# Moving half of the value products into loop one's last batch, rounding the first tensors on VectorE, and giving the key rows their own order in the last FFN part

## The chip, the cores and the metric

One core of one Trainium2 chip. The metric is the time of the device in microseconds for one launch of the whole program. TensorE is called PE here, VectorE DVE, ScalarE ACT, GpSimd POOL, SyncE SP; SP issues nearly all the DMAs.

## The reference

Two decoder layers on x (8 batches, 512 rows, 256 channels), with a context of 64 rows per batch. All in float32:

```
x = LN(x + linear_attention(x));  x = LN(x + cross_attention(x, ctx))
x = LN(x + FFN(x))      # FFN: up, gate, sigmoid, t and v are rounded to 16 bits,
                        # each by the maximum of its absolute value over ALL 8 batches
x = LN(x + metric_attention(x))
x = LN(x + cosine_attention(x, ctx))   # k, v = ctx @ Wkv; 16 heads of 64; k = l2norm(k) * k_scale
x = LN(spectral(x) + bias)
```

The global maxima divide the program: no value of a tensor can be rounded until the maximum over all batches is known. Two things of the second layer depend on the context alone and are worked out ahead of it: the scaled, normalised keys (`ck_d`, four groups of 128 context rows) and the products of the values with the output weights (`vw_d`). The values come in 8 pairs of heads (`values(p)`), and each pair gives 2 units (`value_products(n)`, n from 0 to 15).

## The kernel before, in words

Every engine runs a list of its own, written out by hand, and the lists meet at semaphores. `unrolled(engine, steps)` takes a list of (skew, step) pairs and in round n calls each step for batch n minus its skew. An engine takes its instructions strictly in the order of the list, and so does SP's queue.

1. **Loop one** (to 367 us): linear and cross attention for the 8 batches. The last rounds hold batch 7 alone: `xat_turn_probs`, `xat_denominators`, `xat_spread`, `xat_values`, `xat_project_o` on PE. Then the three FFN weights are turned (`turn`, L894), while DVE normalises batch 7, finds the maximum of x and rounds x.
2. **Gate pass** (380 to 474 us): x is turned and multiplied with the gate weights, batch by batch (L911, L922).
3. **Up part** (487 to 590 us): `up_pass(u)` on PE; ACT rounds the gate (`gate_round`, L1406), takes the sigmoid (`ffn_sigmoid`, L1411) and copies the up products (L1399); DVE multiplies and looks for maxima (`gate_product`, `t_peak`, `up_peak`). Between them PE works out `values(0)` to `values(2)` and `value_products(0)` to `(5)` (L979, L1000). ACT copies them (`copy_values` L1438, `copy_vw` L1448) into one buffer (`vw_at`, three from unit 11 on), and SP stores each unit in two DMAs (`store_vw`, L560).
4. **Last FFN part** (604 to 692 us): ACT rounds t and up of the batch `V_ORDER[q]` (`ffn_round_t` L1501, `ffn_round_up` L1509), DVE multiplies them and takes the maximum (`product(q)`, L2056 and L2059). SP loads up for q+2 once ACT has rounded q, and stores the product. PE and ACT do `values(3)` to `(7)`, units 6 to 15, and the keys: `key_rows(g)` on PE (L1014), `copy_keys(g)` (ACT, L1520), a square on POOL (L1726), `sum_keys(g)` on DVE (L2068), a power and a product on POOL (L1728, L1731), `turn_keys(g)` on PE (L1022), `store_keys(g)` (ACT, L1531, with its own DMA).
5. **Loop two** (692 us to the end): down projection, metric, cosine and spectral parts for the 8 batches. Before it DVE waits until all the keys are stored, and PE until they are scaled.

The lists of this kernel follow.

## Time and profile before

| | us |
|---|---|
| median of three runs | 1440.66 (1438.76 to 1443.44) |
| profiled execution, its own time | 1441.74 |
| its span | 1439.4 |
| PE busy | 1256.5 (87%) |
| DVE busy | 1039.9 (72%) |
| ACT busy | 518.6 (36%) |
| POOL busy | 274.1 (19%) |

The busy shares are means over parts with different limits. In the row "PEclk" of the page each digit is the clock that PE was granted in a fortieth of the span, in tenths: 9 is the full 2.4 GHz within rounding, and 7 or 6 means that PE spent part of the slice at 1.2 GHz. The low digits lie where loop one ends and in the last FFN part.

### The profile page before, as it was taken

The page shows a single profiled execution, that of the slowest core. Times are in us where ns is not written, and L with a number is a line of the kernel's source. Part 1 is how long each engine was busy: PE and PEld are TensorE (multiplying, and loading weights), DVE is VectorE, ACT ScalarE, POOL GpSimd, SP SyncE. Part 2 cuts the span into 40 slices and gives each one's busy share as a digit, 9 for nine tenths or more (in the row PEclk, how much of TensorE's full clock was granted, in tenths as well). Part 3 has the DMA queues.
Part 4 walks back from the last instruction along what each step waited for, and adds up shares of the span by engine and source line. Part 5 has one row for each costly group of instructions (what it writes and reads, how often), then busy time and mean ns, then how long its engine had stood idle before and what let it go on. Part 6 is the DMA issues. An engine that isn't in the chain of part 4 may idle for free.

```text
span 1439.4 us, 18378 instructions
## 1 busy us (share of the span) xinstructions
PE 1256.5 (87%) x7324; PEld 837.9 (58%) x7324; DVE 1039.9 (72%) x1925; ACT 518.6 (36%) x602; POOL 274.1 (19%) x188
## 2 busy tenths in 40 slices
PE   7899999977699999664568999999999999998964
PEld 4565666655444544332456576867767686766653
DVE  3579889986346488786543597987879797878684
ACT  1234334433234577677011423332233333241410
POOL 0011111110000000054100230414132141414140
PEclk9899999998899999877699999999999999999997
DMA  5000000000251146498220210021111000000000
GB/s 209 15 15 31 30 30 30 16 15 16 106 217 59 74 155 216 146 386 305 91 83 17 92 51 31 30 68 44 52 59 51 30 23 24 29 22 25 1 15 15
DMA packets 47060, 105.23 MB, mean 73 GB/s; under 512 B 10496, under 2 KB 31104, under 8 KB 43648
## 3 DMA queue, kind: packets, MB, share of 16 engines
q1 hardware_dynamic: 42816, 101.96, 20.1%
q10 hardware_dynamic: 4160, 2.10, 0.5%
q8 instruction: 58, 0.95, 0.3%
q14 instruction: 26, 0.21, 0.0%
HBM read 60.01 MB, written 44.04 MB: 72 GB/s over the span
## 4 chain that ended last, share of the span: by engine, by line
PE 74%; DVE 16%; ACT 5%; issue 3%; DMA 1%; POOL 1%; SPq 0%; POOLq 0%; DVEq 0%; ACTq 0%
PE ps L1197 7%; PE ps L1257 7%; PE ps L1086 6%; PE ps L922 6%; PE ps L973 5%; PE ps L733 3%; PE ps L1230 3%; PE ps L1144 3%; PE ps L877 2%; PE ps L1168 2%; PE ps L806 2%; PE ps L1179 2%; PE ps L824 2%; PE ps L1274 2%; PE ps L713 2%
## 5 line engine op out<-in xcount | busy, mean ns | idle before, releaser
L1257 PE MATMUL ps<-arena 128*128 128x256 f32 x512 | 119.9, 389 | 6.7 <-ACT arena L1654 6.7
L1197 PE MATMUL ps<-arena 128*128 128x512 f32 x256 | 117.6, 598 | 0.0
L1257 PEld LDWEIGHTS ps<-arena 128*128 128x128 f32 x512 | 98.7, 195 | 27.8 <-ACT arena L1654 10.2
L1681 POOL TENSOR_TENSOR arena<-arena 128x4 f32<-128x4 f32 x48 | 49.4, 1032 | 340.8 <-DVE arena L1839 340.8
L1086 PE MATMUL ps<-arena 128*128 128x256 f32 x384 | 89.7, 394 | 22.6 <-DVE arena L2100 20.4
L2145 DVE TENSOR_TENSOR arena<-ps,arena 128x2048 f32<-128x2048 f32 x32 | 73.3, 2292 | 39.3 <-PE ps L1144 39.1
L1745 POOL TENSOR_TENSOR arena<-arena 128x16 f32<-128x16 f32 x32 | 91.9, 2906 | 34.1 <-DVE arena L2174 34.1
L1086 PEld LDWEIGHTS ps<-arena 128*128 128x128 f32 x384 | 75.2, 199 | 33.9 <-issue 20.8
L922 PE MATMUL ps<-arena 128*128 128x512 f32 x192 | 86.1, 606 | 1.2 <-ACT arena L1373 1.2
L973 PE MATMUL ps<-arena 128*128 128x512 f32 x192 | 85.0, 596 | 1.4 <-ACT arena L1399 1.4
L1197 PEld LDWEIGHTS ps<-arena 128*128 128x128 f32 x256 | 46.3, 190 | 48.1 <-issue 44.5
L1633 ACT ACTIVATE arena<-ps 128x512 f32<-128x512 f32 x64 | 38.3, 599 | 98.2 <-PE ps L1197 98.2
L1654 ACT ACTIVATE arena<-ps 128x1024 f32<-128x1024 f32 x32 | 32.8, 1026 | 110.3 <-PE ps L1244 110.3
L1845 DVE TENSOR_SCALAR arena<-arena 128x256 f32<-128x256 f32 x192 | 67.4, 416 | 7.0 <-POOL arena L1681 7.0
L1230 PE MATMUL ps<-arena 128*128 128x128 f32 x512 | 63.3, 277 | 6.0 <-DVE arena L2188 6.0
L1688 POOL TENSOR_TENSOR arena<-arena 128x1024 f32<-128x1024 f32 x8 | 18.8, 2353 | 246.6 <-DVE arena L1899 246.6
L1230 PEld LDWEIGHTS ps<-arena 128*128 128x128 f32 x512 | 60.4, 192 | 8.3 <-DVE arena L2188 7.6
L922 PEld LDWEIGHTS ps<-arena 128*128 128x128 f32 x192 | 36.8, 195 | 45.0 <-issue 43.2
L973 PEld LDWEIGHTS ps<-arena 128*128 128x128 f32 x192 | 36.1, 190 | 45.6 <-issue 40.5
L733 PE MATMUL ps<-arena 128*128 128x512 f32 x128 | 59.2, 597 | 1.3 <-ACT arena L1307 1.3
L1992 DVE TENSOR_REDUCE arena<-arena 128x1 f32<-128x3072 f32 (+1 forms) x9 | 26.9, 2994 | 39.6 <-issue 39.6
L1833 DVE BATCH_NORM_STATS2 arena<-arena 128x6 f32<-128x256 f32 x144 | 51.8, 415 | 4.5 <-POOL arena L1688 2.6
(247 smaller groups left out, 2639.0 us busy)
## 6 DMA issues: line engine op xcount, KB each, us to landing
v_scratch<-arena SPq DMA_DIRECT2D x7, 1536.0 KB, 8.8
arena<-v_scratch SPq DMA_DIRECT2D x7, 1536.0 KB, 6.8
up_scratch<-arena SPq DMA_DIRECT2D x6, 1536.0 KB, 7.0
arena<-up_scratch SPq DMA_DIRECT2D x6, 1536.0 KB, 9.7
arena<-x_scratch SPq DMA_DIRECT2D x16, 512.0 KB, 4.0
vw_scratch<-arena SPq DMA_DIRECT2D x32, 256.0 KB, 5.0
arena<-vw_scratch SPq DMA_DIRECT2D x8, 1024.0 KB
arena<-x SPq DMA_DIRECT2D x8, 512.0 KB, 5.5
```

The lines of the kernel that those rows point to most:

```text
L733: last = mm(flat(t % 2), lin_xt[:, par, k, t * P:(t + 1) * P], w["lin_wkv"][:, k], start=k == 0, stop=k == NC - 1)
L922: last = mm(flat(2 + j), wgate_t[:, k, j * P:(j + 1) * P], ffn_xt[:, par, k], start=k == 0, stop=k == NC - 1)
L973: last = mm(flat(2 + n % 4), wup_t[:, k, j * P:(j + 1) * P], ffn_xt[:, u % 2, k], start=k == 0, stop=k == NC - 1)
L1086: last = mm(rows2(5)[:, t], dn_v[:, t, j], wdown_t[:, j], start=j == 0, stop=j == NF - 1)
L1197: last = mm(flat(p % 2), w["cos_wq"][:, k, p * P:(p + 1) * P], xt4[:, k], start=k == 0, stop=k == NC - 1)
L1230: last = mm(flat(0, 2)[:, p * P:(p + 1) * P], cos_q[:, p, t * P:(t + 1) * P], cos_kb[:, par, p], start=True, stop=True)
L1257: last = mm(flat(2)[:, C:2 * C], cos_pt[:, p], cos_vw[:, par, p], start=p == 0, stop=p == NP - 1)
L1681: g.tensor_tensor(var[0], var[1], neghalf[:, 0:NT], ALU.pow)\
L1745: g.tensor_tensor(cos_nn[:, t, 0:H], cos_nn[:, t, 0:H], neghalf[:, 0:H], ALU.pow)\
L1833: v.bn_stats(st[:, t], r[:, t])
L1845: last = v.tensor_scalar(y[:, t], r[:, t], mv[:, t, 0:1], rs[:, t:t + 1], ALU.subtract, ALU.mult)
L2145: v.tensor_tensor(met_s[:, n % 2].rearrange("p r t h n -> p (r t h) n"), flat(3, 4).rearrange("p (h n) -> p h n", n=P), w["causal"].unsque ...
```

## The change

Values 0 to 3 and units 0 to 7 move into loop one's last batch and into the turning of the weights. For them SP loads the context, the value weights, the output weights and one column of `pack_prep` early, into room that loop one's last batch has left; the copies go to three buffers. Values 4 to 6 and units 8 to 13 take the places in the up part that 0 to 2 and 0 to 5 had; values 7 and units 14 and 15 alone are left in the last FFN part. The first gate rounding is done by DVE in two halves, and the sigmoid of batch 0 follows in halves; the first t rounding is done by DVE. The key rows are squared by ACT from PSUM, their banks move by one, and DVE sums them after q = 2, 3, 5, 6. Loop two's waits for the keys move from its head to the first `met_mask_states` (DVE) and the first `met_scores(0)` (PE). The gate weights are turned into the banks that the up weights used, once these are copied.

```diff
-        VW_LATER = 11
+        VW_AHEAD = 8
+        AHEAD_V_BANK = (2, 2, 0, 1)
+        AHEAD_VW_BANK = (0, 0, 4, 4, 2, 2, 2, 2)
         def vw_at(n):
-            return 0 if n < VW_LATER else (n - VW_LATER + 1) % 3
+            return 1 + n % 3 if n < VW_AHEAD else 0
...
# SP, loop one
+            def load_values_ahead(b, par):
+                if b.last():
...
+                    sp.dma_start(null_raw, pack_prep[:, prep_at:prep_at + 2]).then_inc(loaded["pack_prep"], 16)
...
+                    sp.dma_start(early_ctx.rearrange("p a b -> p (a b)"), ctx_d).then_inc(ev("ctx_again_loaded"), 16)
...
+                        sp.dma_start(early_wv[k], pack_wv[:, k * INNER:(k + 1) * INNER])\
...
+                    wait(sp, "lin_q_ready", b)
+                    sp.dma_start(early_wo.rearrange("p a b -> p (a b)"), pack_l1[:, wo_at:wo_at + NP * C])\
...
-            unrolled(sp, [(0, load_x), (3, load_ahead), (3, store_x3)])
+            unrolled(sp, [(0, load_x), (2, load_values_ahead), (3, store_ahead(0, 1, 2)), (3, load_ahead),
+                          (3, store_ahead(3, 4, 5)), (3, store_x3)])
+            store_vw(6)
+            store_vw(7)
# PE, loop one: values_ahead(p) is 2 products of 128x512, products_ahead(n) 4 of 64x256
+                (3, products_ahead(0)), (3, values_ahead(1)), (2, lin_out(3)), (1, lin_project_kv(0)),
...
+                (3, products_ahead(1)), (1, lin_project_kv(2)), (3, xat_denominators), (3, products_ahead(2)), (2, lin_turn_y), (1, lin_project_kv(3)),
+                (2, xat_project_q), (3, xat_spread), (2, xat_scores(0)), (3, products_ahead(3)), (3, xat_values),
+                (3, values_ahead(2)), (2, xat_scores(1)), (3, xat_project_o), (2, xat_turn_probs(0)), (0, lin_turn_x), (2, xat_scores(2)), (1, lin_state),
+                (2, xat_turn_probs(1)), (2, values_ahead(0)), (2, xat_scores(3)), (1, lin_out(0))])
...
             turn(4, "w_up", NF, NC)
-            wait(pe, "xat_out_added", Batch(B - 1))
-            turn(0, "w_gate", NF, NC)
+            values_ahead(3)(final, 1)
+            products_ahead(4)(final, 1)
             pe.wait_ge(ev("weight_copied"), WEIGHTS["w_up"])
+            turn(4, "w_gate", NF, NC)
+            products_ahead(5)(final, 1)
+            products_ahead(6)(final, 1)
+            pe.wait_ge(ev("weight_copied"), WEIGHTS["w_gate"])
             turn(4, "w_down", NC, NF)
+            products_ahead(7)(final, 1)
# ACT: copy_values_ahead and copy_vw_ahead stand behind xat_exp and the copies in the same order
# ACT, first sigmoid
+            def first_sigmoid():
+                half = NF * T // 2
+                act.wait_ge(ev("half_gate_rounded"), 1)
+                f(gated[:, 0, 0:half], gate_i[:, 0, 0:half], ACT.Sigmoid, scale=quant["gate_scale"])\
...
-            gate_round(0)
-            ffn_sigmoid(0)
+            first_sigmoid()
# ACT, last FFN part, whole new list
+            copy_values(7), copy_vw(14), ffn_round_up(0), ffn_round_up(1), copy_vw(15), ffn_round_t(1),
+            ffn_round_up(2), ffn_round_t(2), copy_keys(0), ffn_round_up(3), ffn_round_t(3), ffn_round_up(4),
+            copy_keys(1), ffn_round_t(4), ffn_round_up(5), ffn_round_t(5), store_keys(0), ffn_round_up(6),
+            copy_keys(2), ffn_round_t(6), store_keys(1), ffn_round_up(7), copy_keys(3), ffn_round_t(7),
+            store_keys(2), store_keys(3)
# ACT, copy_keys
+                if g:
+                    act.wait_ge(ev("cos_k_summed"), g)
+                f(ksq, flat(1 + 2 * (g % 2), 2), ACT.Square).then_inc(ev("cos_k_squared"), 1)
# POOL
-                g.tensor_tensor(ksq, row, row, ALU.mult).then_inc(ev("cos_k_squared"), 1)
# DVE
-                wait(dve, "t_rounded", Batch(q))
+                if q == 0:
+                    link(v.tensor_scalar(t_i[:, 0], gated[:, at], quant["t_mult"], None, ALU.mult))
+                else:
+                    wait(dve, "t_rounded", Batch(q - 1))
...
-                if 1 <= q <= 4:
-                    sum_keys(q - 1)
+                if q in (2, 3, 5, 6):
+                    sum_keys((2, 3, 5, 6).index(q))
...
-            dve.wait_ge(ev("ck_stored"), 16 * 4)
# DVE, met_mask_states; PE's wait for cos_k_scaled moves likewise to met_scores(0)
+                if b.first():
+                    dve.wait_ge(ev("ck_stored"), 16 * 4)
```

(The new ACT list is written here with commas; in the file each call has a line.)

## Rows read from the trace of the kernel before

**Rows 1.** Busy time of each engine in the last FFN part, by stretch.
```profile
core 0: us, PE busy (x) PEld busy (x) DVE busy (x) ACT busy (x) POOL busy (x), PEclk, DMA share, GB/s
...
604.22:692.66 88.44, 43.85 (x145) 21.22 (x143) 65.11 (x49) 60.85 (x36) 36.90 (x13) 0.73 0.87 313
```

**Rows 2.** The chain of waits, 600 to 613 us: start, length, what.
```profile
601.45 4.55 ACT arena L1509 x2
...
606.84 2.85 ACT arena L1501
...
609.71 3.36 DVE arena L2056
```

**Rows 3.** Groups by line and shape, 600 to 692 us: busy, mean ns, idle before.
```profile
L2056 DVE TENSOR_TENSOR arena<-arena 128x3072 f32<-128x3072 int16 x8 | 26.9, 3357 | 15.8 <-ACT arena L1501 15.7
L2059 DVE TENSOR_REDUCE arena<-arena 128x1 f32<-128x3072 f32 x8 | 26.8, 3348 | 0.3
L1501 ACT ACTIVATE arena<-arena 128x3072 int16<-128x3072 f32 x8 | 22.8, 2846 | 0.6 <-ACT arena L1531 0.6
L1509 ACT ACTIVATE arena<-arena 128x3072 int16<-128x3072 f32 x8 | 22.7, 2852 | 10.4 <-DVE arena L2056 10.4
L1014 PE MATMUL ps<-arena 128*128 128x512 f32 x32 | 20.3, 793 | 4.3 <-ACT arena L1531 4.3
L1728 POOL TENSOR_TENSOR arena<-arena 128x16 f32<-128x16 f32 x4 | 17.7, 4437 | 6.4 <-DVE arena L2069 6.4
...
L1448 ACT ACTIVATE arena<-ps 128x1024 f32<-128x1024 f32 x10 | 10.2, 1016 | 4.5 <-DMA vw_scratch<-arena 4.4
...
L2068 DVE TENSOR_REDUCE arena<-arena 128x16 f32<-128x1024 f32 x4 | 4.9, 1220 | 9.8 <-POOL arena L1726 9.8
```

**Rows 4.** DMA issues: KB of each, median us from issue to landing.
```profile
v_scratch<-arena SPq DMA_DIRECT2D x7, 1536.0 KB, 8.8
...
arena<-up_scratch SPq DMA_DIRECT2D x6, 1536.0 KB, 9.7
```

**Rows 5.** PE in time, end of loop one: start, length; idle before in brackets.
```profile
290.71 1.95 PE L866 MATMUL ps<-arena 128*128 128x128 f32 x16
...
349.45 1.24 PE L824 MATMUL ps<-arena 128*128 128x128 f32 x8 [2.74 <-ACT arena L1339]
351.81 3.64 PE L842 MATMUL ps<-arena 128*32 128x128 f32 x64 [1.11 <-ACT arena L1346]
356.53 3.78 PE L866 MATMUL ps<-arena 128*128 128x128 f32 x16 [1.08 <-DVE arena L1927]
...
363.69 3.72 PE L877 MATMUL ps<-arena 128*128 128x256 f32 x16 [1.41 <-DVE arena L1933]
...
380.17 1.94 PE L911 MATMUL ps<-arena 128*128 128x128 f32 x8 [8.32 <-DVE arena L1983]
```

**Rows 6.** Busy time by stretch, columns as in rows 1, around loop one's end.
```profile
349.45:367.25 17.80, 14.19 (x121) 10.84 (x122) 4.90 (x5) 2.05 (x2) 2.00 (x1) 0.71 0.24 90
...
380.17:390.93 10.76, 9.59 (x22) 4.88 (x23) 2.66 (x4) 1.02 (x1) 0.00 (x0) 0.64 0.27 98
```

**Rows 7.** PE in time, up part: the first wait, one values, one unit.
```profile
487.34 3.70 PE L973 MATMUL ps<-arena 128*128 128x512 f32 x8 [1.39 <-ACT arena L1399]
...
521.84 1.88 PE L979 MATMUL ps<-arena 128*128 128x512 f32 x4
...
536.98 1.13 PE L1000 MATMUL ps<-arena 64*128 64x256 f32 x8 [1.69 <-ACT arena L1448]
```

**Rows 8.** ACT in time at the first sigmoid.
```profile
481.53 1.28 ACT L1411 ACT_TABLE_LOAD   x1
482.83 2.85 ACT L1411 ACTIVATE arena<-arena 128x3072 f32<-128x3072 int16 x1
```

**Rows 9.** DVE in time, the first scaling of a sigmoid.
```profile
485.78 1.76 DVE L2022 TENSOR_SCALAR arena<-arena 128x3072 uint16<-128x3072 f32 x1 [6.97 <-ACT arena L1411]
```

**Rows 10.** POOL in time, the power of the third key group.
```profile
650.32 2.90 POOL L1728 TENSOR_TENSOR arena<-arena 128x16 f32<-128x16 f32 x1 [1.60 <-DVE arena L2069]
```

More of the change, by code:

```diff
@@ L325, in decoder @@
         kst = ar.take(NP, P)
-        vw_bufs = (vw_out, ar.take(2, 2, C), ar.take(2, 2, C))
+        ar.at = lin_x_at
+        early_wv = [ar.take(INNER)]
+        early_vst = (ar.take(B * TC), ar.take(B * TC))
+        ar.at = lin_xt_at
+        early_wv.append(ar.take(INNER))
+        early_ctx = ar.take(NC, B * TC)
+        ar.at = lin_zq_at
+        early_wo = ar.take(NP, C)
+        ar.at = lin_z_at
+        vw_bufs = [vw_out, ar.take(2, 2, C), ar.take(2, 2, C)]
+        ar.at = lin_ek_at
+        vw_bufs.append(ar.take(2, 2, C))
+        assert keep + 3 * NF * T <= lin_x_at and ar.at <= keep + B * NF * T
+        null_raw = small[:, 42:44]
         ar.at = keep
@@ L863, in xat_spread @@
                 wait_behind(pe, "xat_spread_copied", b, 1, 1, 1)
+                if b.last():
+                    pe.wait_ge(ev("vw_copied"), 2)
                 for c in range(NC):
@@ L879, in xat_project_o, with values_ahead, step @@
                 last.then_inc(sig("xat_out_projected").sem, 1)
+            def values_ahead(p):
+                def step(b, par):
+                    if not b.last():
+                        return
+                    if p == 0:
+                        pe.wait_ge(ev("ctx_again_loaded"), 16)
+                        pe.wait_ge(loaded["pack_wv"], 16 * NC)
+                        wait_behind(pe, "xat_out_added", b, 1, 1, 1)
+                    elif p == 1:
+                        pe.wait_ge(ev("cos_v_copied"), 1)
+                    else:
+                        wait(pe, "xat_spread_copied", b)
+                    for k in range(NC):
+                        last = mm(flat(AHEAD_V_BANK[p]), early_wv[k][:, p * P:(p + 1) * P], early_ctx[:, k],
+                                  start=k == 0, stop=k == NC - 1)
+                    last.then_inc(ev("cos_v_projected"), 1)
+                return step
@@ new lines, in products_ahead, with step @@
+            def products_ahead(n):
+                p = n // 2
+                def step(b, par):
+                    if not b.last():
+                        return
+                    pe.wait_ge(ev("cos_v_copied"), p + 1)
+                    if n == 0:
+                        pe.wait_ge(loaded["pack_l1"], 16)
+                        wait_behind(pe, "xat_spread_copied", b, 1, 1, 1)
+                    elif n == 2:
+                        wait(pe, "xat_shifted", b, NT, NT)
+                    elif n == 4:
+                        wait(pe, "xat_out_added", b)
+                    else:
+                        pe.wait_ge(ev("vw_copied"), n)
+                    for i in range(2):
+                        at = (2 * (n % 2) + i) * P
+                        for r, (lo, hi) in enumerate(((0, CD), (CD, P))):
+                            last = mm(flat(AHEAD_VW_BANK[n] + r)[:, i * C:(i + 1) * C],
+                                      early_vst[p % 2][lo:hi, at:at + P], early_wo[lo:hi, p], start=True, stop=True)
+                    last.then_inc(ev("vw_done"), 1)
+                return step
@@ L918, in step @@
                     for j in range(half * NF // 2, (half + 1) * NF // 2):
-                        if not b.first():
+                        if b.first():
+                            pe.wait_ge(ev("vw_copied"), VW_AHEAD)
+                        else:
                             wait(pe, "gate_copied", b, j + 1 - NF, NF)
@@ L1377, in ffn_copy_gate @@
                 g_b = gated[:, b.off].rearrange("p (t j n) -> p t j n", t=NT, j=NF)
+                if b.off == 3:
+                    for n in range(VW_AHEAD - 3, VW_AHEAD):
+                        act.wait_ge(vw_line(n), 32 * vw_before(n) + 32)
                 for j in range(NF):
@@ L1530, in store_keys @@
                     act.wait_ge(ev("ck_stored"), 16 * g)
-                f(kst.rearrange("p a b -> p (a b)"), flat(2 + 2 * (g % 2), 2), ACT.Copy, scale=gk)\
+                f(kst.rearrange("p a b -> p (a b)"), flat(1 + 2 * (g % 2), 2), ACT.Copy, scale=gk)\
                     .then_inc(ev("cos_k_scaled"), 1)
@@ L2037, in up_peak @@
                 link(v.tensor_tensor(quant["up_max"], quant["up_max"], peaks[:, 0:1], ALU.max))
-            for n in range(B - 1):
+            first_gate_product()
+            t_peak(0)
+            up_peak(0)
+            for n in range(1, B - 1):
                 gate_product(n)
```

279 lines of the change are left out of this document (156 added, 123 removed).

## Prediction

> **What bounds the kernel now.** I read the page's clock row first: PE holds nearly its full clock except where loop one ends and in the last FFN part. Then I cut the span into stages by busy time. In the last FFN part, 88.44 us long, no engine is full: PE 43.85, DVE 65.11, ACT 60.85, and the DMA engines are at 0.87 [rows 1]. The chain of waits says what order does there: ACT rounds two up tensors, then t, and only then does DVE begin its first product at 609.71 [rows 2]. From there to the last maximum DVE needs 8 products (3.357) and 8 maxima (3.348) [rows 3]; yet it is idle 15.8 us before products, for ACT's t rounding, and 9.8 before key sums, for POOL's square [rows 3]. So the stage is held by the order of ACT's list, not by any engine's work.
>
> At the end of loop one PE waits again and again: 2.74 us for an exponential, 1.11, 1.08 and 1.41 after it, and 8.32 before the first turn of the gate pass [rows 5]. It also works at a mean granted clock of 0.71 from 349.45 to 367.25, and 0.64 from 380.17 to 390.93 [rows 6]; 0.5 is 1.2 GHz, 1.0 is 2.4. The same 16 instructions of L866 take 1.95 in the round before and 3.78 here [rows 5].
>
> All terms are set against the profiled execution, 1441.74 (span 1439.4 and 2.3 around it), which stands 1.08 above the median 1440.66.
>
> **Part A, values and units in the drain of loop one.** Added on PE: 4 values at 1.88 (a record's length, of which some 0.16 overlaps the next, so 1.72) and 8 units at 1.13, with the same overlap 1.06 [rows 7]: 4 x 1.72 + 8 x 1.06 = 15.4 us. ACT gets 4 copies of 512 and 8 of 1024 elements; the latter take 1.016 [rows 3]. The former I put at two thirds of that, 0.7; they can't be below 0 nor above 1.016. Together 11 us. Where they fall:
> - values 0, unit 0 and values 1 (4.5 us) lie in the waits for batch 7's exponentials, of which the last alone is 2.74 [rows 5] and the one before it in the same rhythm is as long. Unit 1 lies in the 1.11 before L842, unit 2 in the 1.08 before L866 [rows 5]. Nothing of these on the path.
> - unit 3 stands ahead of `xat_values`, with no wait there to cover it: +1.06. Values 2 (1.72) stands ahead of `xat_project_o`, whose wait for DVE is 1.41 [rows 5]: +0.3.
> - values 3, units 4 to 7 (1.72 + 4.2 = 6.0) and the turns of the gate and down weights lie beside DVE's normalising, the maximum of x and its sharing, 12.7 us from the end of `xat_project_o` to 380.17. Step by step, counting from that end: up weights turned at 1.3, unit 4 at 4.1, gate weights at 5.4, unit 5 at 6.5, unit 6 at 8.9 (after ACT's copies), down weights at 10.2, unit 7 at 11.3, ACT's last copy at 12.6. It fits by 0.1. What is late if it doesn't fit is the first turn, one for one.
> - the clock. Each fall of PE's clock stood behind waits like these. With the waits filled, PE has hardly a gap over 1.5 us until loop one's end, and I take the clock as kept. L842 then takes half of 3.64, -1.8; L866 takes 1.95 for 3.78, -1.8 [rows 5]. So `xat_project_o` comes at 1.06 + 0.3 - 3.6 = -2.2. Likewise for the gate pass's start: 9.59 busy at clock 0.64 is 6.1 at full clock, -3.4 [rows 6]. Part A: -5.6. Bounds: -7 (the copies' room also shortens something), and +2.5 if the clock falls as before (no saving, unit 2 doubles and outgrows its wait by 1.0, +1.4 from above; the 3.4 stays too), up to +6 if the three-buffer chain of copy and store is late as well.
> - SP: the new loads, 2.5 MB, are issued behind batch 5's store and have some 20 us until they are needed; an up load of 1.5 MB lands in 9.7 [rows 4]. The last x3 store comes behind the stores of units 3 to 5, about 3 us later than before, but only batch 7's later load reads it, and the load of batch 2, behind it in the queue, is issued at the first turn as before. Nothing.
>
> **Part B, first gate rounding.** ACT's rounding and its sigmoid go one after the other, with a table load of 1.28 between, and PE's fifth up product then waits 1.39 for ACT's first copy [rows 7, 8]. DVE's half should take half of 1.76 [rows 9], 0.9; then the table, then two half sigmoids of 1.4: ACT is free 1.9 us sooner, PE's wait of 1.39 goes, and PE paces the up part from there. -1.4. Bounds: 0, if the table is loaded late and halves carry a fixed cost; -1.9.
>
> The Trainium skill (ScalarE: Activation LUTs, "What ACT_TABLE_LOAD costs") charges a switch of tables 2.66 us, the load and a drain. Here the sigmoid starts 0.02 after the 1.28 of the load [rows 8]: this trace has no such drain. By the rule Part B would be -0.5, by the row -1.4.
>
> The places of units 8 to 13 in the up part are those of units 0 to 5, with one buffer again: the 1.69 wait per pair [rows 7] stays, no change.
>
> **Part C, the last FFN part.** The head: DVE rounds t of q = 0 itself (1.76 as in [rows 9], while ACT rounds up), so product 0 waits for ACT's first up rounding alone. In the chain two roundings start at 601.45 and 606.84 is where t's began [rows 2]; the first ends at 604.2. 609.71 - 604.2 = 5.5 sooner.
>
> The pace: a round of DVE is 3.36 + 3.35 + 0.16 and gaps = 6.98; eight are 55.8; four key sums of 1.22 and a small one, 1.45 each, are 5.8: 61.6 against the 79.8 that it took from 609.71 to 689.5 (the stage's end at 692.66 [rows 1], less 3.2 for the last scale and roundings). Units 6 to 13 and values 3 to 6 leave ACT (8 x 1.0 + 4 x 0.7 = 11 us), and four squares come to it (L1448's 1.016 is the nearest row, the same shape from PSUM; at least 0, at most 2). ACT's list is then 15 roundings started every 2.75, 41, plus units 14 and 15 and values 7, 8 key copies and squares, 4 scaled stores: 57 in all, under DVE's 61.6. What still stalls DVE: round 3 by the wait of `copy_keys(0)` for v's first store (8.8 [rows 4] from 609), 0.7; the last key group, where `key_rows(3)` (8 x 0.793 = 6.3 at most [rows 3]) waits for `store_keys(1)`, so that t(7) comes 2.4 late; POOL's product, which held a one-element DVE operation for 1.2 in two of the rounds. I put 4.3. So 79.8 - 61.6 - 4.3 = -13.9, and with the head -19.4.
>
> Bounds: with no stall -23.7; with 8 us more of stalls (half of the 15.8 + 9.8 [rows 3] that there were, less what I count) -11.5. The DMA engines move 88.44 x 313 = 27.7 MB [rows 1]; 16 unit stores of 0.26 go, so 23.5 MB are left for 67 us, 350 GB/s. It ran at about that rate. In order of issue the loads for q = 5, 6 and 7 come 1 to 3 us before ACT wants them.
>
> **Part D, the waits of loop two.** The last key store would land some 8 us after `store_keys(3)`, about when DVE ends or 10 us later; its first readers are 40 us into loop two. Moved, it costs 0. Left where it was, it would have cost up to 10, which is why it must be counted with Part C.
>
> Sum: 1441.74 - 5.6 - 1.4 - 19.4 = 1415.3; less 1.08 for the median, **1414**.
>
> **The rivals.**
> 1. *The clock falls at loop one's end all the same.* The work put in is short pieces, and 2.74 and 8.32 were not the only gaps. Against it: those gaps are the ones filled. Part A +2.5 for -5.6: **1422**.
> 2. *DMA paces the last FFN part.* For it: 0.87 busy over the whole stage [rows 1], and a round of 7 to 8 us asks for 1.5 MB in and 1.5 MB out. If it moves 313 GB/s as before, 23.5 MB take 75 us from 604, 8 more than I give: **1422 to 1424**.
> 3. *POOL's power holds DVE's products.* POOL's L1728 took 4.437 in the mean [rows 3] against 2.90 for the third group, which had begun before DVE's product [rows 10]: POOL waits for DVE. The other way round nothing shows: 8 products have a mean of 3.357 [rows 3]. If each of four products waited 2.9, that is 11.6 less the 2.4 counted: **1423**. The Trainium skill (SBUF — State Buffer, "Who interferes with whom") calls the shared port an exclusive lock of whoever starts first, which would bring this about where the power starts first.
> 4. *The key groups run behind DVE's list: slower than before.* `sum_keys(g)` stands in DVE's order, and DVE stops there until ACT has squared the group, which needs a free bank, hence the store of group g-2, hence POOL's power and product of that group. Before, DVE waited 9.8 for four sums [rows 3]. If each group misses its place by more than a round, 26.4 / 4 = 6.6 us beyond what I count is where it decides; at 8.5 us each, +34: **1448**. Against it: from copy to scaled store a group took 16 us, and the places are 7 to 15 us apart with two groups in flight.
> 5. *The moved units don't take anything off the path*, since ACT waited for t in its own order: then only the head and Part B count, 1441.74 - 5.5 - 1.4 - 1.1: **1434**. Against it: the 15.8 us idle ends at ACT's L1501 [rows 3], with unit copies ahead of it in the list.
>
> **How the numbers follow.** My forecast 0.52 (its own range 1410 to 1418), rival 1 0.22, rivals 2 and 3 together 0.14, rival 5 0.04, rival 4 0.03; 0.05 below 1410, where the stalls vanish. 8 in 10: 1408 to 1427. 0.3% of this kernel is 4.3 us, about what its measurement can tell from no change. Faster 0.96, same 0.015, slower 0.025.
>
> **What would show it.** PE's L842 near 1.9 and L866 near 1.95 in batch 7, and a clock near 1.0 from 349 to 390 (Part A, against rival 1); PE's 1.39 wait gone (B); the first L2056 about 5.5 us after the last scale and the eight of them within 66 us; DVE idle before L2056 under 5 us, not named DMA (C, rival 2); L2056 with a mean still 3.36 (rival 3); idle before L2068 under 4 (rival 4); no idle of DVE or PE for the keys in loop two (D). It is wrong if the gate pass starts no sooner than 380, or if the stage from the last up product to loop two is over 80 us.

## The result and the profile after

The changed kernel takes 1428.53 us in the median of four runs (1426.56 to 1429.01), the kernel before, measured beside it, 1442.05 (1438.76 to 1444.49): a ratio of 0.9903, 95% interval 0.9885 to 0.9922. It is faster by 13.5 us. The forecast was 1414, a gain of 26.7, in a range of 1408 to 1427: the direction was right, half of the size is missing, and the time lies outside the range. The profiled execution took 1429.01, span 1427.2, against 1441.74 and 1439.4 before.

First the end of loop one, PE in time (start, length; idle before and what ended it). These rows answer to [rows 5]: L888 is the old L842, L914 the old L866, L927 the old L877, L1012 the old L911 and L1025 the gate pass.

```profile
350.35 1.96 PE L888 MATMUL ps<-arena 128*32 128x128 f32 x64 [0.22 <-ACT arena L1439]
...
353.38 2.05 PE L914 MATMUL ps<-arena 128*128 128x128 f32 x16
...
360.12 3.62 PE L927 MATMUL ps<-arena 128*128 128x256 f32 x16
...
371.84 1.14 PE L968 MATMUL ps<-arena 64*128 64x256 f32 x8 [1.48 <-ACT arena L1472]
...
376.54 1.07 PE L1012 MATMUL ps<-arena 128*128 128x128 f32 x8 [1.05 <-DVE arena L2101]
378.79 7.11 PE L1025 MATMUL ps<-arena 128*128 128x512 f32 x12 [1.17 <-ACT arena L1502]
385.74 1.04 PE L1012 MATMUL ps<-arena 128*128 128x128 f32 x8
```

The clock beside it, by stretch (columns as in [rows 1]; the number after the bracket of POOL is the granted clock). The first stretch answers to the first of [rows 6]: 1.00 instead of 0.71. In the gate pass the clock still fell, two stretches of 2 us show it at 0.71 and at 0.50, the lower level of 1.2 GHz.

```profile
350.35:363.57 13.22, 13.20 (x133) 9.18 (x133) 4.75 (x4) 4.62 (x5) 0.00 (x0) 1.00 0.79 221
...
378.00:380.00 2.00, 1.22 (x2) 0.70 (x3) 0.00 (x0) 0.73 (x1) 0.00 (x0) 0.71 0.84 245
380.00:382.00 2.00, 2.00 (x3) 0.77 (x3) 0.00 (x0) 0.00 (x0) 0.00 (x0) 0.50 0.74 184
```

Then the last FFN part, groups by line and shape from 592 to 678 (busy, mean ns, idle before). L2195 is DVE's product, the old L2056; L2207 the key sum, the old L2068; L1665 ACT's scaled key copy, ahead of its store.

```profile
L2195 DVE TENSOR_TENSOR arena<-arena 128x3072 f32<-128x3072 int16 x8 | 26.9, 3358 | 5.7 <-ACT arena L1632 3.5 <-ACT arena L1640 2.1
...
L2207 DVE TENSOR_REDUCE arena<-arena 128x16 f32<-128x1024 f32 x4 | 4.9, 1219 | 7.5 <-ACT arena L1654 7.4
L1665 ACT ACTIVATE arena<-ps,arena 128x1024 f32<-128x1024 f32 x4 | 4.5, 1114 | 10.7 <-PE ps L1125 6.2 <-DMA ck_scratch<-arena 4.5
```

DVE's idle time before products fell from 15.8 to 5.7, before key sums only from 9.8 to 7.5 [rows 3], and almost all of the latter is one wait of 7.43. DVE in time, product 3 and the last key group:

```profile
621.79 3.36 DVE L2195 TENSOR_TENSOR arena<-arena 128x3072 f32<-128x3072 int16 x1 [1.83 <-ACT arena L1632]
...
661.43 1.22 DVE L2207 TENSOR_REDUCE arena<-arena 128x16 f32<-128x1024 f32 x1 [7.43 <-ACT arena L1654]
```

The chain of waits (start, length, what) says what it hung on:

```profile
597.60 3.36 DVE arena L2195
...
635.59 15.80 DMA ck_scratch<-arena
651.48 1.12 ACT arena L1665
652.65 6.73 PE ps L1117 x8
659.43 0.89 issue
660.32 1.02 ACT arena L1654
661.34 2.75 ACT arena L1632
664.11 3.36 DVE arena L2195
667.51 3.36 DVE arena L2198
670.90 0.17 DVE arena L2199
671.09 0.16 DVE arena L2079
671.25 3.89 issue
675.15 0.39 POOL arena L1824
...
678.00 12.90 PE ps L1177 x48
```

Read it from below. Loop two begins at 678.00 (692.66 before). POOL shares v's maximum at 675.15, 3.9 us after DVE had it, in a pause that the trace puts to nothing ("issue"); before, the share came 0.1 us behind the end of DVE's copy. The last product stands at 664.11 behind ACT's rounding, that behind the square of key group 3, that behind PE's key rows, these behind the scaled copy that `store_keys(1)` begins with, and this behind the landing of the first key store, which took 15.80 us.

Both traces side by side, each stretch after less before. The measured column adds to the change of the span, -12.2, but for rounding:

| stretch | forecast | measured |
|---|---|---|
| loop one to batch 7, the same work in both | 0 | -1.4 |
| Part A, to the second turn of the gate pass (390.77, 385.74) | -5.6 | -3.6 |
| Part B, to the last unit pair of the up part (590.18, 583.49) | -1.4 | -1.7 |
| head of Part C, to the first product (609.71, 597.60) | -5.5 | -5.4 |
| its pace, first product to last maximum (79.8, 73.5) | -13.9 | -6.3 |
| last maximum to loop two (3.15, 6.91) | 0 | +3.8 |
| loop two (746.7, 749.2) | 0 | +2.5 |

### The profile page after: what moved, and what is told of

It is laid out like the page before. It is cut to its first block, busy times and chain, and to the rows that moved or that the text cites. A ratio compares the mean times of both kernels' runs of the same rounds, so it can differ in the third digit from the quotient of the medians.

```text
span 1427.2 us, 18392 instructions
## 1 busy us (share of the span) xinstructions
PE 1249.9 (88%) x7324; PEld 832.9 (58%) x7324; DVE 1042.0 (73%) x1930; ACT 516.8 (36%) x605; POOL 263.7 (18%) x184
## 4 chain that ended last, share of the span: by engine, by line
PE 74%; DVE 15%; ACT 4%; issue 3%; DMA 2%; POOL 1%; SPq 0%; POOLq 0%; DVEq 0%; ACTq 0%
PE ps L1290 8%; PE ps L1350 7%; PE ps L1177 6%; PE ps L1025 6%; PE ps L1076 6%; PE ps L779 3%; PE ps L1323 3%; PE ps L1237 3%; PE ps L927 2%; PE ps L1261 2%; PE ps L852 2%; PE ps L1272 2%; PE ps L1367 2%; PE ps L870 2%; PE ps L1337 2%
## 5 line engine op out<-in xcount | busy, mean ns | idle before, releaser
L1025 PE MATMUL ps<-arena 128*128 128x512 f32 x192 | 85.5, 602 | 1.2 <-ACT arena L1502 1.2
L1025 PEld LDWEIGHTS ps<-arena 128*128 128x128 f32 x192 | 36.5, 193 | 44.6 <-issue 42.9
```

The lines of the kernel that those rows point to most:

```text
L1025: last = mm(flat(2 + j), wgate_t[:, k, j * P:(j + 1) * P], ffn_xt[:, par, k], start=k == 0, stop=k == NC - 1)
```

## The experiments

The runs of one kernel lie up to 8 us apart (e11_all, 1410.84 to 1418.75), and in the traces the first batches of loop one, which are the same in all, end up to 5 us apart: the unit behind PE's wait of 1.48, at 371.84 above, stands between 368.80 and 374.07 in the eleven traces that have it besides. I call its start the mark. Beside the median (of four runs; of two for e3_thin_v) I read the distance from this mark to the first product and to the first down projection of loop two, and the length from there to the end:

| kernel | median us | ratio to before, 95% | first product | loop two | its length |
|---|---|---|---|---|---|
| changed kernel | 1428.53 | 0.9885 to 0.9922 | 225.8 | 306.2 | 749.2 |
| e1_two_stages | 1419.83 | 0.9808 to 0.9853 | 226.7 | 300.8 | 748.5 |
| e2_share_first | 1433.64 | 0.9909 to 0.9956 | 226.2 | 312.0 | 747.9 |
| e3_thin_v | 1423.89 | 0.9839 to 0.9893 | 225.9 | 300.7 | 748.5 |
| e5_pool_square | 1427.8 | 0.9865 to 0.991 | 225.8 | 306.9 | 749.4 |
| e6_gate_act | 1428.81 | 0.9885 to 0.9918 | 229.0 | 307.5 | 748.5 |
| e7_t0_act | 1426.15 | 0.9867 to 0.9899 | 231.4 | 306.1 | 749.5 |
| e9_keys_after | 1414.45 | 0.9779 to 0.9815 | 225.9 | 292.5 | 749.3 |
| e10_fills | 1425.11 | 0.9854 to 0.9904 | 226.2 | 305.9 | 747.1 |
| e11_all | 1415.2 | 0.9777 to 0.9828 | 227.1 | 296.0 | 747.2 |
| e12_best | 1412.07 | 0.9773 to 0.9803 | 228.1 | 294.7 | 747.9 |
| e13_keys_t0 | 1418.9 | 0.9802 to 0.9864 | 231.6 | 298.2 | 747.7 |

In e6_gate_act and e12_best both distances hold 1.7 us that no edit put there. Behind a unit of the up part PE's clock fell once, and 24 products took 12.26 us in place of 10.57. PE in time and by stretch, e6_gate_act:

```profile
558.61 1.13 PE L1102 MATMUL ps<-arena 64*128 64x256 f32 x8 [1.69 <-ACT arena L1573]
559.68 12.26 PE L1076 MATMUL ps<-arena 128*128 128x512 f32 x24
...
560.00:562.00 2.00, 2.00 (x3) 0.70 (x3) 2.00 (x1) 1.21 (x1) 0.00 (x0) 0.50 1.05 237
```

The same happens in e12_best at 529.28 and in e8_before_fill at 556.96, and in no other of the fourteen traces, though each has two such waits of 1.69, a unit and 24 products behind each.

**The wait for the key store: e1_two_stages.** Two stages, in the room of the value weights, and two semaphore lines for their stores. The room being another, `store_keys(0)` no longer waits for v's products and stores either; ACT had not been idle ahead of it in the changed kernel.

```diff
-        kst = ar.take(NP, P)
+        kst = [wv_all[:, k * NP * P:(k + 1) * NP * P].rearrange("p (a b) -> p a b", a=NP) for k in range(2)]
...
-                    act.wait_ge(ev("ck_stored"), 16 * g)
+                if g >= 2:
+                    act.wait_ge(ck_line(g), ck_at(g - 2))
```

> The changed kernel with two staging tiles for the scaled keys, in the room of the value weights, in place of one. Theory 1 (one staging tile): in the changed kernel ACT waits 4.45 us at 647 for the first key store to land, 15.8 us after its issue, and the fourth group's rows, its square, its sum (DVE idle 7.4 us) and the last t rounding stand behind that. With two tiles the wait goes: store_keys(1) near 647, the last product near 659 instead of 664.1, loop two's first down projection near 672.7 instead of 678.0, so about 5 us less. Theory 2 (DMA paces the part): ACT then waits as long for the next up load or v store, and the gain is under 1 us. Theory 3 (PE's key_rows at 6.7 us each pace it): gain 2 us or less.

Measured 1419.83, 8.7 less than the changed kernel. ACT's second scaled copy came at 646.79 instead of 651.48 though the first store took 15.4 us again; DVE in time (start, length; idle before) shows the last group's sum waiting 1.53 instead of 7.43:

```profile
655.42 1.22 DVE L2214 TENSOR_REDUCE arena<-arena 128x16 f32<-128x1024 f32 x1 [1.53 <-ACT arena L1663]
...
658.10 3.36 DVE L2202 TENSOR_TENSOR arena<-arena 128x3072 f32<-128x3072 int16 x1 [1.25 <-ACT arena L1641]
```

Loop two begins 5.4 us sooner from the mark, as theory 1 had it (about 5). From the first product to the last maximum it is 66.9 us in place of 73.5: that one wait was the larger part of the 7.6 that the pace lacked.

**Why the store lands so late: e3_thin_v.** The same single stage; this kernel leaves out three quarters of v's bytes, in these stores and in loop two's loads, so its output is not the reference's.

```diff
-                sp.dma_start(v_rows[V_ORDER[q]], gated[:, V_ORDER[q]].rearrange("p (t n) -> p t n", t=NT))\
+                sp.dma_start(v_rows[V_ORDER[q]][:, 0:1], gated[:, V_ORDER[q]].rearrange("p (t n) -> p t n", t=NT)[:, 0:1])\
```

> The changed kernel with the stores of the last FFN product, and their loads in loop two, cut to the first quarter of the rows, so the output is not the reference's; all waits stay. Theory 1 (the DMA engines are full in the last FFN part): the first key store lands in under 6 us instead of 15.8, ACT's wait of 3.9 us for the first v store goes, up loads land in 7 us instead of 10.2, and the last FFN part is 6 to 9 us shorter. Theory 2 (the key stores are slow by their own 512-byte pieces): their landing stays over 10 us and the part gains 3 us at most, from the v wait.

The longest of the four key stores took 7.7 us instead of 15.8, and none is waited for. So the store was late because it was issued into the traffic of v's stores and up's loads. Theory 1 has the cause; its figures, a landing under 6 us and a part 6 to 9 us shorter, were not reached, and ACT's wait for the first v store fell to 1.76 from 3.92, it did not go. Loop two begins 5.4 us sooner from the mark, as in e1_two_stages, but not by the same sum: first product to last maximum is 65.9 us, 1.0 less than there, while POOL's power and product of group 3 end at 663.17, level with DVE's last maximum, and its pause puts loop two 8.9 behind that maximum (7.2 in e1_two_stages).

**The share of v's maximum: e2_share_first.** POOL shares it ahead of group 3's power and product.

```diff
                 pool.wait_ge(ev("cos_k_summed"), g_at + 1)
+                if g_at == 3:
+                    share_peak("v")
...
-            share_peak("v")
```

> The changed kernel with POOL's sharing of v's maximum ahead of the last key group's power and product, not behind them. Theory 1 (POOL needs some 5.5 to 6 us between an ordinary operation and the sharing, 5.92 in the changed kernel, 5.47 for x's maximum in the kernel before): POOL has then been idle for long when DVE has the maximum, the sharing starts within 0.3 us of it instead of 3.9, and loop two starts 3.6 to 3.9 us sooner; the last key store is later by 8 to 12 us and nobody waits for it. Theory 2 (the 3.9 us belong to the sharing itself or to its semaphore): no change, or slower by what the keys are later. Theory 3: ACT or PE reach loop two late because the last key group is late: slower by 2 to 5.

Slower than the changed kernel by 5.1 in the median, by 5.9 from the mark. POOL in time:

```profile
671.90 0.38 POOL L1824 PARTITION_ALL_REDUCE arena<-arena  x1 [15.27 <-DVE arena L2080]
679.35 2.95 POOL L1848 TENSOR_TENSOR arena<-arena 128x16 f32<-128x16 f32 x1 [7.07 <-issue]
```

The share starts 0.2 us behind the end of DVE's copy (671.67), but POOL pays on the way back as well: 7.07 us to the power of group 3, whose sum had been ready since 663.28. And group 3's turn lies ahead of loop two in PE's list, so PE stood still until 684.33: the first half of theory 1 and the end of theory 3.

**Both ends: e9_keys_after.** e1_two_stages, the share ahead of group 3, and all of group 3 past the end: ACT copies it behind t(7), DVE sums it behind loop two's first roundings, PE turns it behind the first down projection (the two new steps of loop two act in batch 0 alone; of their two lists only the places with the new step are printed).

```diff
             turn_keys(2)
-            turn_keys(3)
...
+                (0, dn_project(3)), (0, last_keys_turn),
...
+            ffn_round_t(7)
             copy_keys(3)
-            ffn_round_t(7)
...
-                if q in (2, 3, 5, 6):
+                if q in (2, 3, 5):
...
+                (0, dn_round(3)), (0, last_keys_sum),
```

> The changed kernel with the two key stages of e1_two_stages, and with the last key group taken past the end of the last FFN part: ScalarE copies and squares it behind t(7)'s rounding, VectorE sums it behind loop two's first roundings, GpSimd shares v's maximum ahead of its power and product, TensorE turns it behind the first down projection. Theory 1 (the maximum is shared late because GpSimd's ordinary work of group 3 lies just ahead of it, and the last product is late because ScalarE's copy and square of group 3 lie ahead of t(7)): against e1_two_stages the last product starts at about 654.5 instead of 658.10 (no wait of 1.53 and 1.25 and no sum of 1.39 on VectorE), the share follows the last maximum in under 1 us instead of 4.3, and TensorE's loop two starts at about 664.7 instead of 672.27; in all some 7.5 us less than e1_two_stages, so near 1412. Theory 2 (the gap ahead of the share belongs to the share, whatever ran before): GpSimd still takes some 6 us there and loop two starts at about 668.5, near 1416. Theory 3 (what is taken off here comes back: the keys' turn and store now lie in loop two, and its first round waits for them, or its transfers for a late store): loop two starts early but TensorE's rows of its second round stand less than 4 us earlier than in e1_two_stages, the time stays within 2 us of 1420.

1414.45, between the 1412 of theory 1 and the 1416 of theory 2; but loop two begins at 664.53 where theory 1 had 664.7, and its length is that of the changed kernel. PE and POOL in time:

```profile
664.53 12.89 PE L1185 MATMUL ps<-arena 128*128 128x256 f32 x48 [9.03 <-DVE arena L2247]
677.25 1.04 PE L1134 MATMUL ps<-arena 128*128 128x128 f32 x8
```
```profile
661.67 0.38 POOL L1834 PARTITION_ALL_REDUCE arena<-arena  x1 [7.32 <-DVE arena L2090]
669.27 2.95 POOL L1858 TENSOR_TENSOR arena<-arena 128x16 f32<-128x16 f32 x1 [7.22 <-DVE arena L2219]
```

The share starts 0.1 us behind the end of DVE's copy (661.53), and from the last maximum to loop two it is 3.15 us again, as before the change: with 7.32 us behind its last ordinary operation POOL's pause costs nothing. The 7.22 behind the share are no pause but a wait for DVE's sum of group 3, which ends at 669.08, and nobody waits for them. 14.1 us less than the changed kernel in the medians, 13.6 from the mark; against e1_two_stages 8.2 from the mark, of which 3.4 came in the pace (63.5 for 66.9), 4.0 behind the last maximum and 0.8 ahead of the first product. What each of the moved steps gave of this was not taken apart.

**PE's clock at loop one's end: e8_before_fill.** The kernel before, with seven products of constants in batch 7's waits and nothing else.

```diff
+            def filler(n, first=False):
...
+                        for _ in range(n):
+                            mm(flat(2), w["lin_wq"][:, 0, 0:P], w["lin_wkv"][:, 0], start=True, stop=True)
```

> The kernel before with products of constants (never read) put into PE's waits of batch 7 in loop one: 2, 3, 1 and 1 of them, 6 us at full clock. No other work is moved. Theory 1 (clock): PE's clock stays at full through the denominators and the spread, L842 and L866 take 1.9 each instead of 3.64 and 3.78, xat_project_o comes 3.4 to 3.7 us sooner and so does everything behind it: total 3.5 less. Theory 2 (the changed kernel's 2.2 us in this place came from elsewhere, the clock falls all the same): no gain, up to 2 us slower where a filler at half clock outgrows its wait.

1437.16 against 1441.67, ratio 0.9957 (0.9941 to 0.9974). The same two groups as in [rows 5]:

```profile
347.67 1.96 PE L842 MATMUL ps<-arena 128*32 128x128 f32 x64 [0.25 <-ACT arena L1355]
...
350.70 2.05 PE L866 MATMUL ps<-arena 128*128 128x128 f32 x16
```

Measured from L866 of the round before (286.72 here, 290.71 there), `xat_project_o` comes 3.7 us sooner, 3.4 of it in the two halved groups. The granted clock is 1.00 from 347 to 361 us. PE's clock had been lost behind its waits, and both kinds of work put into them, units of the product and products of constants, kept it. The wait of 8.41 ahead of the gate pass was left empty here, and there nothing was gained: the clock is 0.66 from 372 to 384, and the first twelve products take 7.55 (7.65 before).

**The gate pass and loop two's start: e10_fills, e11_all, e12_best.** Products of constants there: two and two around the first turn of the gate pass, and eight behind the last v product (e10_fills, e11_all) or seven behind key group 2 (e12_best). `fill(n)` issues n products of 128x512. e11_all and e12_best are e9_keys_after with these, and with ACT's copy of group 0 behind up(3)'s rounding.

```diff
+            fill(2)
             pe.wait_ge(ev("weight_copied"), WEIGHTS["w_down"])
...
+                if b.first():
+                    fill(2)
...
+            wait(pe, "v_ready", Batch(B - 1))
+            for _ in range(8):
+                mm(flat(0), late_ctx[:, 0, 0:P], late_ctx[:, 0], start=True, stop=True)
```

> The changed kernel with products of constants in TensorE's waits: two behind the last product of the units, two behind the first turn of the gate pass, eight behind the last v product ahead of loop two (no result of theirs is used). Theory 1 (TensorE's granted clock falls because it idles in these places; that ate 2 us of the gate pass's forecast gain and about 1 of loop two's start): the twelve products of the first gate round take about 5.4 to 6.2 us instead of 7.11, the first down projection of loop two about 11 instead of 12.9, the time falls by 2 to 4 us, to near 1425. Theory 2 (the fall comes of the units' own mixed load, or is not to be helped by so little): both lengths stay, time 1428.5. Theory 3 (the fillers themselves run at the low clock and hold up what follows): up to 4 us more, 1430 to 1432.

PE in time, e10_fills:

```profile
374.35 1.98 PE L1007 MATMUL ps<-arena 128*128 128x512 f32 x4 [1.39 <-ACT arena L1484]
376.17 1.04 PE L1019 MATMUL ps<-arena 128*128 128x128 f32 x8
377.04 1.88 PE L1007 MATMUL ps<-arena 128*128 128x512 f32 x4
378.76 5.31 PE L1034 MATMUL ps<-arena 128*128 128x512 f32 x12
...
666.52 8.81 PE L1173 MATMUL ps<-arena 128*128 128x512 f32 x16
675.17 10.52 PE L1189 MATMUL ps<-arena 128*128 128x256 f32 x48
```

The twelve products take 5.31 instead of 7.11, but the fillers hold the first turn up: it stands 6.88 behind the mark instead of 4.70. The second turn is 14.62 behind it instead of 13.90, 0.7 lost. Ahead of loop two the down projection takes 10.52 instead of 12.89 and starts about 1.6 behind VectorE's first rounded rows (673.56). The median fell by 3.4, but this trace has its mark 2.6 sooner; from the mark to the end it is 2.4 shorter, 0.3 of it ahead of loop two. That is the 2 to 4 us of theory 1, but no more than traces differ by without an edit (loop two alone by 3.6, see below).

> All of it in one kernel: two key stages, the last key group past the end (as e9_keys_after), ScalarE's copy of group 0 behind up(3)'s rounding, and the products of constants of e10_fills (no result of these is used). If the parts add: e9_keys_after's time less what e10_fills takes off (2 to 4 us) and less up to 1.8 for product 3, which waited 1.83 us behind the copy of group 0: near 1408. Rival: with t(3) earlier VectorE is only held at the next load of up or the next store of v, and the fillers ahead of loop two find too short a wait to matter: then the same as e9_keys_after, 1411 to 1413.

1415.2, no better than e9_keys_after. The fillers ended at 669.6 where VectorE's first rows were ready at 667.2, and what the projection gained was paid ahead of it. Product 3's wait was gone, but DVE lost 1.2 in another place, where POOL held its one-element maximum (1.38 us; the last section has such a case).

> e11_all with seven products of constants ahead of loop two instead of eight, and put right behind the turn of key group 2 instead of behind the last v product (no result of theirs is used). In e11_all they ended at 669.6, some 2.4 us after VectorE had the first rows ready, so that what the faster down projection gave (10.52 us instead of 12.89) was paid ahead of it. Theory 1 (both ends can be had): they end before the first rows are ready, the 48 products of the down projection stay near 10.6 us, and the time is 3 to 4 us below e9_keys_after: 1410 to 1411. Theory 2 (the clock falls again in the wait between them and the projection, or the seven still run into it): projection over 12 us or late, time as e9_keys_after less the gate pass's 1.7: 1412 to 1413.

```profile
654.54 6.17 PE L1180 MATMUL ps<-arena 128*128 128x512 f32 x14
663.74 13.56 PE L1196 MATMUL ps<-arena 128*128 128x256 f32 x48 [3.02 <-DVE arena L2258]
```

Theory 2: PE idled 3.02 behind the fillers, and the projection took 13.56. 1412.07 is the lowest median of all. From the mark loop two begins 2.2 later than in e9_keys_after, 1.7 of it by the fall of the clock in the up part, and the intervals of the two overlap; I count them as equal, and e9_keys_after as the plainer design.

**ScalarE's part: e5_pool_square, e6_gate_act, e7_t0_act, e13_keys_t0.** Each takes back one edit.

```diff
-                f(ksq, flat(1 + 2 * (g % 2), 2), ACT.Square).then_inc(ev("cos_k_squared"), 1)
+                g.tensor_tensor(ksq, row, row, ALU.mult).then_inc(ev("cos_k_squared"), 1)
```

(e5_pool_square, on GpSimd.)

```diff
-            first_gate_product()
-            first_sigmoid()
+            gate_round(0)
+            ffn_sigmoid(0)
```

(e6_gate_act, both new lines in ScalarE's list.)

```diff
-                    link(v.tensor_scalar(t_i[:, 0], gated[:, at], quant["t_mult"], None, ALU.mult))
+            ffn_round_t(0)
```

(e7_t0_act and e13_keys_t0, ScalarE's list, behind `ffn_round_up(1)`.)

> The changed kernel with the squares of the key rows back on GpSimd (2.2 to 3.3 us each there, 1.02 on ScalarE). Theory 1 (ScalarE is the engine that paces the last FFN part once VectorE has lost its first rounding; four squares of 1.02 are taken off it, but each sum comes later by GpSimd's square, and for group 3 that lies on the path): products 3, 4, 6 start up to 1 us earlier, but group 3's sum, power, product and with them the share and loop two come some 1 to 2 us later: 1428 to 1431, within the noise of the changed kernel. Theory 2 (GpSimd's work holds VectorE up, as I gave a chance in the forecast): VectorE's products beside the squares are longer than 3.36 us and the time is 4 or more us longer, 1433. Theory 3 (ScalarE is what matters): 3 to 4 us less, 1425.

1427.8, loop two 0.7 later from the mark, nearest to theory 1 (1 to 2 later). A square took 1.90 on POOL, not 2.2 to 3.3. POOL's power took 5.9 in three of four groups instead of one, and ACT waited 7.3 for the key store instead of 4.5: with that wait in place the square's place decides nothing, and without it nothing was tried.

> The changed kernel with the gate's first rounding and first sigmoid as before: both on ScalarE, whole, behind each other, VectorE's list without the first gate product. Theory 1 (the head of the up part was bound by this chain, and the trace's net gain of 1.65 us is all of it): TensorE idles about 1.4 us before up product 5 as it did before, the up part ends some 1.7 us later, the time is 1430.2. Theory 2 (the early table load did it, not the split rounding): the load stays early, at most 0.5 us is lost, 1428.5 to 1429. Theory 3 (what is lost at the head is waited for again by the loads of up at its end): no change in the time, though the first rows are later.

Part B undone, PE idles 1.29 ahead of up product 5 again. The unit ahead of the fall of the clock stands 1.66 later from the mark, the 1.7 of theory 1; with the fall's 1.7 the first product stands 3.3 later (229.0 for 225.8). Yet loop two begins only 1.4 later and the median is the same. DVE's wait for the last key group is 4.82 instead of 7.43: what is lost ahead was partly waited for anyway.

> The changed kernel with t(0)'s rounding back on ScalarE, where it was. Theory 1 (ScalarE has the longer list in the head of the last FFN part): the first product starts about 1 us later (ScalarE's 2.75 for t(0) against VectorE's 1.81), and ScalarE's list is 2.75 longer, which its later waits for a v store and the key store partly hide: 1 to 3 us more, 1430 to 1431. Theory 2 (VectorE is the bound there, one rounding of 1.81 less for it): up to 1 us less, 1427.5. Theory 3 (ScalarE's whole list lies on the path up to the first key store's landing): the full 2.75 more, 1431.3 or above.

Not as any of the three had it. The first product stands 5.7 later and loop two where it was; the median is even 2.4 lower, no more than the first batches differ by (the mark stands 2.1 sooner in this trace). ACT in time:

```profile
634.83 0.59 ACTq L1668 DMA_DIRECT2D ck_scratch<-arena  x1
```

The first key store is issued 1.3 later from the mark than in the changed kernel and falls otherwise between v's stores and up's loads, which I take for the reason without a test of it: none of the four takes more than 11.3, and ACT waits 0.4 instead of 4.5. The last product comes at 658.95, 3.1 sooner from the mark; then POOL's ordinary work and its pause set the start of loop two, 8.8 behind the last turn of the keys as in the changed kernel (8.7).

> e9_keys_after (1414.45, no wait for a key store and none for the last group) with t(0)'s rounding back on ScalarE. In e7_t0_act the same edit on the changed kernel put the first product 5.3 us later, and yet the time fell by 2.4. Theory 1 (the head's gain is real, and in the changed kernel the key store, which lands late when it is issued beside big transfers, took it back; with that wait gone it stands): the first product starts some 3.6 to 5.3 us later than in e9_keys_after, VectorE then goes without a pause, product 3's wait of 1.22 gone, and loop two starts 2.4 to 4.1 us later: 1417 to 1418.5. Theory 2 (the first product's place does not matter, the later loads of up and stores of v set the pace whenever it starts): no more than 1 us later at loop two, 1414.5 to 1415.5.

With those waits out of the way (e9_keys_after) the same edit costs 4.4 in the median (1418.9, runs from 1416.2 to 1421.6) and 5.6 from the mark, more than the 2.4 to 4.1 of theory 1. The head's gain is real, and the changed kernel could not keep it.

## Why the forecast was half right

**Part A (-5.6, measured -3.6).** The first half came as worked out: the two halved groups took 3.4 off, the work ahead of `xat_project_o` put 1.2 on, and it stands 2.2 sooner; e8_before_fill shows the clock alone as the cause of the 3.4. The units beside DVE's normalising cost nothing: the first turn stands 16.42 behind `xat_project_o`, 16.48 before. The step that failed is the second half, "-3.4" at the gate pass: I took its clock as kept since "PE has hardly a gap over 1.5 us". Behind gaps of 1.48, 1.05 and 1.17 it fell all the same, to 0.50 at 380; 1.4 came. In e10_fills, with products in the last two, it stayed at 1.00 from 376 to 384.

**Part B (-1.4, measured -1.7).** Right in size. The table load stood early, in ACT's wait for the scale. e6_gate_act gives it again, 1.66; the rest of its 3.3 at the first product is the clock's fall shown above.

**Part C, head (-5.5, measured -5.4).** Right, and e13_keys_t0 gives it again, 5.7 at the first product and 5.6 at loop two.

**Part C, pace (-13.9, measured -6.3).** The step that failed is the term of stalls, "I put 4.3", and in it the last key group, "so that t(7) comes 2.4 late". DVE waited 7.43 for that group's square and 1.25 for t(7). The step named `store_keys(1)` but not the landing it waits for; the one key landing that the prediction prices is the last, at some 8 us, and the first took 15.8 beside transfers of 1.5 MB. `key_rows(3)` behind it took 6.7 where 6.3 was put as the most. The other stalls were 1.83 at product 3 for the 0.7 forecast (v's first store, issued at 602.42, held ACT until 614.34), 1.17 where POOL held a one-element maximum, for the two of 1.2 forecast, and 0.41 at product 6: 12.1 in all for the 4.3. The wait for the first key store stood in ACT's order, and ACT's order was what held this stage. With it gone the pace is 66.9 (e1_two_stages, 598.17 to 665.08), and with the last group out too 63.5 (e9_keys_after, 597.89 to 661.38), against the forecast of 65.9. The sign "over 80 us" from the last up product to loop two was misplaced: from PE's last up product it is 104.2 us before, 96.2 after, and by the forecast itself 85.

**The end of the stage (0, measured +3.8).** A step that I didn't have. I took 3.2 from the last maximum to loop two over from before, where POOL had been idle for 19 us. Now its last ordinary operation ended at 669.23, 1.9 ahead of DVE, and the share followed only 5.92 behind that. It is POOL's own end that sets it: in six more traces, too, the share stands 5.82 to 6.20 behind POOL's last operation, whether DVE's maximum had been there for 4 us or for 6, and with POOL done earlier (e9_keys_after) the step is 3.15 again. Bringing the end of one engine forward brought it up against another.

**Part D (0)** stands: neither DVE nor PE waits for keys in loop two, even in e9_keys_after, where the last group is turned there.

**Loop two (0, measured +2.5)** was not touched. Over all fourteen traces its length runs from 746.7 (before) to 750.3 (e8_before_fill, which has the same loop two as before). So the 2.5 are within what two executions of one code differ by; what in it differs was not followed up.

**The rivals.** 1 happened at the gate pass alone, 2.0 of its 8.1. 2: ACT waited 1.6 for loads of up in all; the traffic told in two places, v's first store (3.92, 1.83 of it for DVE) and the key store (e3_thin_v). 3 is refuted as I put it: the products' mean stayed at 3358 ns. 4, at 0.03, had the right mechanism, a key group behind DVE's list, once instead of four times: DVE's idle time before key sums is 7.5, over the 4 that was set as its sign. That the time stayed far from its 1448 is owed to the other three groups, which were in time. 5 is out: the pace is 6.3 shorter even so, and 16.3 in e9_keys_after.

## What to carry to other kernels

When an edit makes a stage faster, list each wait that stands in the order of the engine that paces it, and price it with the traffic of the faster stage, not with a median landing from the slower one; a small store behind big ones is the first to look at, and a second buffer for it is cheap. Then look at what must follow the last instruction of the stage: an engine that had been idle for long may now come late. And where TensorE waits, price what follows at both levels of its clock: at the gate pass it fell behind waits of 1.0 to 1.6 us in every trace of the changed kernel and its variants that had no products of constants there (the first twelve products took 6.94 to 7.11, and 5.31 with them), while behind the waits of 1.69 in the up part it fell in three traces of fourteen. Such a chance fall also sets how far two traces can be compared.

## What the runs showed of the hardware

GpSimd pauses between an ordinary operation and the share over the partitions. Ahead of v's share it is 5.92 in the changed kernel and 5.82 (e6_gate_act) to 6.20 (e1_two_stages) in six more traces; ahead of x's share it is 5.47 (kernel before) to 6.26 (e10_fills). Where POOL has longer to wait for DVE, the share starts 0.1 us behind DVE's copy (7.32 in e9_keys_after, 19.18 in the kernel before). Behind the share one trace shows a pause, 7.07 in e2_share_first; in the others the next operation waited for DVE. What POOL does in the pause no run shows.

GpSimd and VectorE hold each other up in some places. e9_keys_after, POOL's product of group 2 and DVE's one-element maximum, which takes 0.16 otherwise:

```profile
646.49 5.88 POOL L1858 TENSOR_TENSOR arena<-arena 128x16 f32<-128x16 f32 x1 [8.60 <-DVE arena L2219]
652.45 1.90 POOL L1861 TENSOR_TENSOR arena<-arena 128x1024 f32<-128x1024 f32 x1
```
```profile
646.26 3.35 DVE L2206 TENSOR_TENSOR arena<-arena 128x3072 f32<-128x3072 int16 x1
...
653.04 1.33 DVE L2210 TENSOR_TENSOR arena<-arena 128x1 f32<-128x1 f32 x1
654.40 3.36 DVE L2206 TENSOR_TENSOR arena<-arena 128x3072 f32<-128x3072 int16 x1
```

The maximum ends at 654.37, POOL's product at 654.35: DVE was held for 1.2 us. The power, begun 0.23 behind DVE's product, took 5.88 instead of 2.9, longer by 3.0, about what was left of the product. In the changed kernel the power begins 0.27 ahead of DVE's product:

```profile
646.80 2.90 POOL L1846 TENSOR_TENSOR arena<-arena 128x16 f32<-128x16 f32 x1 [8.59 <-DVE arena L2208]
```
```profile
647.07 3.36 DVE L2195 TENSOR_TENSOR arena<-arena 128x3072 f32<-128x3072 int16 x1 [0.41 <-ACT arena L1632]
```

It took 2.90 and the product 3.36: neither held the other. The Trainium skill (SBUF — State Buffer, "Who interferes with whom") has the shared port as a lock of whoever starts first. The first two cases agree with it; in the third, by that rule, the product should have waited, and it did not.
